# Half of the last FFN's tokens sorted by expert instead of run through all eight experts

## The reference

```python
shared = silu(xf @ shared_w1.T) * (xf @ shared_w2.T) @ shared_w3.T      # hidden 512
scores = sigmoid(xf @ router_w.T)                                       # 8 experts
_, top_idx = top_k(scores + expert_bias, 2)
mask = one_hot(top_idx, 8).sum(axis=-2)
gates = scores * mask
h1, h2 = split(einsum('td,ehd->teh', xf, w12), 2)                       # hidden 128 per expert
h = silu(h1) * h2 * gates[:, :, None]
routed = einsum('teh,edh->td', h, w3)
x = x + 0.5 * (shared + routed)
```

## Time and profile before

| | us |
|---|---|
| median of three runs | 722.5 |
| the profiled execution, device time | 724.5 |
| its span, first to last instruction | 722.5 |
| first FFN, first half (0 to 124 us) | TensorE busy 111.4 of 124.0 |
| mamba, sections 1 to 6 (482.6 to 587.5) | TensorE busy 104.4 of 104.9 |
| mamba, last section (587.5 to 604.6) | TensorE busy 14.7 of 17.1 |
| last FFN, start (604.6 to 616.2) | TensorE busy 10.7 of 11.6 |
| last FFN, units (616.2 to 718.0) | TensorE busy 101.5 of 101.8 |

### The profile page before, as it was taken

One profiled execution on the slowest core, in us unless ns is written; L12 is line 12 of the kernel. 1 busy time (PEld: TensorE's weight loads), 2 busy tenths in 40 slices (PEclk: granted clock), 3 DMA queues, 4 the chain that ended last, 5 costly groups with the idle time before them and its releaser, 6 DMA issues. The chain is left out here.

```text
span 722.5 us, 12386 instructions
## 1 busy us (share of the span) xinstructions
PE 677.4 (94%) x4100; PEld 506.3 (70%) x4100; DVE 569.2 (79%) x1308; ACT 419.3 (58%) x757; POOL 324.5 (45%) x404
## 2 busy tenths in 40 slices
PE   7899998797899999999999878999999998999997
PEld 5667774643457777777778676777777775777785
DVE  5789978989978888988989855666766676879774
ACT  4557686885245555556656647555565555455553
POOL 2568884101227766465658461220413200555463
PEclk9999999999999999999999989999999999999999
DMA  6625430000013232222213100000000000323131
GB/s 168 200 89 187 137 110 1 0 1 0 1 52 125 70 108 90 88 59 81 96 59 90 29 1 1 2 2 2 1 2 0 0 1 2 117 74 118 56 122 44
DMA packets 34329, 43.16 MB, mean 60 GB/s; under 512 B 5216, under 2 KB 17504, under 8 KB 34272
## 3 DMA queue, kind: packets, MB, share of 16 engines
q1 hardware_dynamic: 34272, 42.46, 19.1%
HBM read 41.13 MB, written 1.31 MB: 59 GB/s over the span
## 5 line engine op out<-in xcount | busy, mean ns | idle before, releaser
L697 POOL TENSOR_TENSOR p_prod<-p_p,p_gate_row 128x512 f32<-128x512 f32 x128 | 203.5, 1602 | 108.7 <-DVE p_p L504 62.4
L384 ACT ACTIVATE p_sil<-p_ps_a 128x512 f32<-128x512 f32 x176 | 105.3, 598 | 131.1 <-PE p_ps_a L100 126.8
L509 DVE TENSOR_TENSOR p_hlo<-p_prod,p_hhi 128x512 fp32r<-128x512 f32 x176 | 149.6, 851 | 0.3 <-ACT p_hhi L393 0.2
L504 DVE TENSOR_TENSOR p_p<-p_sil,p_ps_b 128x512 f32<-128x512 f32 x128 | 87.1, 681 | 54.3 <-ACT p_sil L384 37.3
L393 ACT CAST p_hhi<-p_prod 128x512 fp32r<-128x512 f32 x176 | 108.1, 615 | 24.9 <-POOL p_prod L697 24.9
L98 PE MATMUL p_ps_a<-xt_hi,w_uphi 128*128 128x512 f32 x176 | 74.2, 422 | 0.0
L98 PE MATMUL p_ps_acc<-p_hhi,w_downhi 128*128 128x512 f32 x176 | 71.1, 404 | 1.2 <-DVE p_hlo L509 1.0
L98 PE MATMUL p_ps_b<-xt_hi,w_uphi 128*128 128x512 f32 x176 | 71.2, 404 | 0.1
L100 PE MATMUL p_ps_a<-xt_hi,w_uplo 128*128 128x512 f32 x176 | 70.1, 398 | 0.0
L99 PE MATMUL p_ps_a<-xt_lo,w_uphi 128*128 128x512 f32 x176 | 70.1, 398 | 0.0
L100 PE MATMUL p_ps_b<-xt_hi,w_uplo 128*128 128x512 f32 x176 | 69.8, 396 | 0.0
(11 more groups left out here) (355 smaller groups left out, 1432.1 us busy)
## 6 DMA issues: line engine op xcount, KB each, us to landing
p_gate_row<-gate_rows SPq DMA_DIRECT2D x128, 256.0 KB, 3.3
w_rawbuf<-in_L_ffn_fc_w_dram SPq DMA_DIRECT2D x3, 512.0 KB, 7.0
w_rawbuf<-in_L_ffn_w_dram SPq DMA_DIRECT2D x3, 512.0 KB, 6.5
out_dram<-x SPq DMA_DIRECT2D x4, 256.0 KB, 3.5
w_rawbuf<-in_L_ffn_shared_w_dram SPq DMA_DIRECT2D x3, 256.0 KB, 5.8
x<-in_L_attn_x_dram SPq DMA_DIRECT2D x2, 256.0 KB, 3.9
x<-in_L_attn_x_dram SPq DMA_DIRECT2D x1, 512.0 KB, 9.2
mb_xraw<-in_L_attn_W_B_dram SPq DMA_DIRECT2D x1, 512.0 KB, 5.0
```

The costliest lines, as they stand in the source:

```text
L384: nc.scalar.activation(sil[:, u % 2], ps_a[:, u % 2], ACT.Silu).then_inc(c["sil"].sem, 1)
L504: nc.vector.tensor_tensor(dst, sil[:, u % 2], ps_b[:, u % 2], ALU.mult).then_inc(c["p1"].sem, 1)
L509: nc.vector.tensor_tensor(hlo[:, u % R], prod[:, u % R], hhi[:, u % R].bitcast(F32), ALU.subtract).then_inc(c["hlo"].sem, 1)
L697: G.tensor_tensor(prod[:, u % R], p1[:, u % 2], gate_row[:, e % ROWS], ALU.mult).then_inc(c["prod"].sem, 1)
```

## The change

The last FFN has a function of its own, `sparse_stream`. Blocks 2 and 3 are computed as before, by 12 units each. Of blocks 0 and 1 (tiles 0 to 7) only the four shared units are computed so. Their experts are done on sorted rows: each of the 1024 tokens is written twice to DRAM, once for each chosen expert, into a list in which each expert's rows begin at a multiple of 128. The list has 23 tiles (`SLOT_TILES = HALF * 2 + EXPERTS - 1`, always all of them computed), in six groups of up to four tiles. Each tile is read back, turned, multiplied by its own expert's weights (whose place in SBUF TensorE has in a register), and written to a second DRAM list, from which each token's two results are gathered and added to x with their gates.

Parts:

1. In mamba, in the two sections that turn blocks 0 and 1: the router's logits on TensorE (12 matmuls), tanh, `choose` on VectorE. In the last section: ranks on TensorE (9 small matmuls), places on VectorE, and at its end GpSimd scatters tiles 0 to 3 (8 indirect DMAs). The norm of block 2 is there too. The loop is written out, its VectorE, ScalarE, GpSimd and TensorE instructions otherwise in the old order.
2. In the first FFN: a blank for the sorted list, 1.5 MB of zeros, is written to DRAM in SyncE's queue.
3. In the last FFN: eight shared units (g = 0 to 7, `CUT` = 8), during which GpSimd scatters tiles 4 to 7 and TensorE loads 23 registers from SBUF; the six sorted groups; then blocks 2 and 3 (g = 8 to 31). `LEAD` is 4 as before; the ring of hidden tiles is 4. In block 2 the experts' gate products alternate between GpSimd and VectorE; the gathers of the results are on GpSimd between its products. The results are added in block 3.

```diff
+    def scatter(self, j):
+        for k in range(2):
+            self.nc.gpsimd.indirect_dma_start(self.rows_dram[:, :], bass.IndirectOffsetOnAxis(ap=self.place[:, k, j:j + 1], axis=0),
+                                              self.xn[:, j], None).then_inc(self.c["z_scat"].sem, 16)
 # mamba, TensorE, step q == 1 of a section
                         if head is not None:
-                            pe.wait_ge(c["xlo"].sem, c["xlo"].at(head + 1))
+                            sort.logits(pe, head, xt, router, ps_y)
+                            outputs(h, m, 0)
+                            pe.wait_ge(c["gth"].sem, c["gth"].at(head + 1))
+                        if not more:
+                            outputs(h, m, 0)
+                            pe.wait_ge(c["z_slot"].sem, c["z_slot"].at(1))
                         tail.to_tokens(pe, m - 1, ps_y)
 # mamba, VectorE
+                    if q == 3 and head is not None:
+                        sort.choose(dve, head)
+                    if q == 0 and not more:
+                        sort.places(dve, ps_y)
+                        sort.owners(dve)
 # mamba, GpSimd, after its last section
+            pool.wait_ge(c["z_place"].sem, c["z_place"].at(1))
+            pool.wait_ge(c["z_blank"].sem, c["z_blank"].at(16))
+            for j in range(SCATTERED):
+                sort.scatter(j)
 # first FFN, SyncE
         def load_rest(sp):
+            sp.dma_start(rows_dram.rearrange("(t p) c -> p t c", p=P), kept["xraw"][:, 0:1].broadcast_to(
+                [P, SLOT_TILES, P])).then_inc(counts["z_blank"].sem, 16)
             w1_set.load(sp, slice(4, None))
             rw_set.load(sp, slice(0, None))
 # last FFN, TensorE
+            def z_up(s):
...
+                for t in range(sizes(s)):
+                    some = bass.ds(owner[s * BT + t] * 2 + S * 2 * P, 2 * P)
+                    last = three_pass_turned(pe, raised(s)[:, t].rearrange("p a c -> p (a c)"),
+                                             [q[s % 2][:, bass.ts(t, P)] for q in (z_xhi, z_xlo)], [q[:, some] for q in up_flat])
...
+            for g in range(CUT):
+                step(g)                     # g == 2: turn_gates(2); g == 7: z_turn_x(0); after each down: z_owners(g)
+            z_turn_x(1)
+            for s in range(GROUPS):
+                z_up(s)
+                if s:
+                    z_turn_h(s - 1)
+                if s >= 2:
+                    z_down(s - 2)
+                if s + 2 < GROUPS:
+                    z_turn_x(s + 2)
+            step(CUT)
+            z_turn_h(GROUPS - 1)
+            z_down(GROUPS - 2)
+            step(CUT + 1)
+            z_down(GROUPS - 1)
+            for g in range(CUT + 2, UNITS):
+                step(g)
 # last FFN, VectorE: the product of p1 waits for the gate product two experts back
+                    dst = p1[:, g % 2]
+                    after(dve, c["prod"], at_expert(g) - 1)
 # last FFN, GpSimd
+            for j in range(SCATTERED, HALF - 1):
+                sort.scatter(j)
+            scale(3)
+            sort.scatter(HALF - 1)
+            weights(2)
+            weights(3)
+            for h in range(2):
+                kept = c[f"z_kept{h}"]
+                pool.wait_ge(kept.sem, kept.at(16 * (GROUPS // 2)))
+            gathered = 0
+            for g in range(FIRST[2] + S, FIRST[2] + U, 2):
+                while gathered < 3 + (g - FIRST[2] - S) // 2:
+                    sort.gather(gathered, z_back)
+                    gathered += 1
+                weigh(g)
 # last FFN, SyncE: rows(2), wait for the scatters, loads and stores of the groups, rows(3), the four stores of x
```

More of the change, by code:

```diff
@@ L100, in three_pass, with three_pass_turned @@
     return pe.matmul(out, weights[1], moving[0], start=False, stop=stop)
+def three_pass_turned(pe, out, tokens, weights):
+    pe.matmul(out, tokens[0], weights[0], start=True, stop=False)
+    pe.matmul(out, tokens[0], weights[1], start=False, stop=False)
+    return pe.matmul(out, tokens[1], weights[0], start=False, stop=True)
 class FfnKind:
@@ L1613 @@
 SPENT = (RWKV_SEMS + [None] * len(MAMBA_SEMS))[:len(MAMBA_SEMS)]
+SPARSE_SPENT = [n for n in MAMBA_SEMS if n not in ("m_yc", "m_sel", "m_yo", "m_yb", "m_yt", "m_yT", "m_yh", "m_yl", "m_ow", "m_out")]
 class MambaHead:
@@ L1785, in add_out, with mamba_phase @@
         self.nc.vector.tensor_tensor(xb, bank[:, 2:4], xb, ALU.add).then_inc(c["m_out"].sem, 1)
-def mamba_phase(nc, counts, spare, sb, ps, x, xt, consts, w, keep, spent, norm, head, tail):
+def mamba_phase(nc, counts, spare, sb, ps, x, xt, consts, w, keep, spent, norm, head, tail, sort, router):
     c = counts
@@ L1939, in turn_head @@
                 for j in range(BT):
-                    last = pe.transpose(bank[:, j], norm["xn"][:, j], ident[:])
+                    last = pe.transpose(bank[:, j], xraw[:, b * BT + j], ident[:])
                 last.then_inc(c["xt"].sem, 1)
@@ L1951, in section @@
                         if head is not None:
-                            pe.wait_ge(c["xlo"].sem, c["xlo"].at(head + 1))
+                            sort.logits(pe, head, xt, router, ps_y)
[4 more added lines that the diff above has]
+                            pe.wait_ge(c["z_slot"].sem, c["z_slot"].at(1))
                         tail.to_tokens(pe, m - 1, ps_y)
-                    if q:
+                    if q > 1 or q and head is None and more:
                         outputs(h, m, q - 1)
-                    elif not first:
+                    elif not q and not first:
                         outputs(1 - h, m - 1, GROUPS - 1)
@@ L2033, in _ @@
             section(0, 2, group=3)
-            with pe.Fori(0, 2) as i:
+            for i in range(2):
                 section(1, i * 2 + 3)
@@ L2083, in section @@
                         bend(m - 1)
+                        if head is not None:
+                            sort.bend(act, head, ps_y)
                     if q == 3 and not first and more:
@@ L2136, in _ @@
             section(0, 2, group=3)
-            with act.Fori(0, 2) as i:
+            for i in range(2):
                 section(1, i * 2 + 3)
@@ L2216, in normal_head @@
                 for j in range(BT):
-                    last = V.scalar_tensor_tensor(out=norm["xn"][:, j], in0=x[:, b * BT + j], scalar=norm["moments"][:, j, 0:1],
+                    last = V.scalar_tensor_tensor(out=xraw[:, b * BT + j], in0=x[:, b * BT + j], scalar=norm["moments"][:, j, 0:1],
                                                   in1=norm["rstd"][:, j:j + 1].broadcast_to([P, P]), op0=ALU.subtract,
@@ L2297, in _ @@
             section(0, 2, group=3)
-            with dve.Fori(0, 2) as i:
+            for i in range(2):
                 section(1, i * 2 + 3, measured=i)
                 section(0, i * 2 + 4, head=i)
-            section(1, BATCH - 1, more=False)
+            section(1, BATCH - 1, more=False, measured=2)
             silu(BATCH - 1)
@@ L2373, in _ @@
             section(0, 2)
+            sort.prepare(pool)
             pool.wait_ge(c["m_grid"].sem, c["m_grid"].at(10))
-            with pool.Fori(0, 2) as i:
+            for i in range(2):
                 section(1, i * 2 + 3, measured=i)
                 section(0, i * 2 + 4)
-            section(1, BATCH - 1, more=False)
+            section(1, BATCH - 1, more=False, measured=2)
+            pool.wait_ge(c["z_place"].sem, c["z_place"].at(1))
+            pool.wait_ge(c["z_blank"].sem, c["z_blank"].at(16))
+            for j in range(SCATTERED):
+                sort.scatter(j)
         @block.sync
@@ L2544, in program @@
             if stage == "mamba":
-                tail = mamba_stage(head)
-            if stage[:3] == "ffn" and (k == 0 or STAGES[k - 1][:3] != "ffn"):
+                tail, sort = mamba_stage(head)
+            if k + 1 == len(STAGES):
+                sparse_stream(nc, f"p{k}", counts, scoped, ps, x, xt, consts, ffn_kind(stage), gate_dram, norm, sort, tail, out_dram,
+                              flat, kept["zs"], kept["xraw"])
+            elif stage[:3] == "ffn" and (k == 0 or STAGES[k - 1][:3] != "ffn"):
                 stages = [stage]
```

673 lines of the change are left out of this document (669 added, 4 removed).

## The result

| | us |
|---|---|
| before, median of 4 runs beside it | 721.88 (721.24 to 723.5) |
| after, median of 4 runs | 740.77 (739.43 to 741.76) |
| ratio, 95% interval | 1.0257 (1.0231 to 1.0283) |
| the profiled execution of after, its span | 741.76, 740.0 |
| its mean TensorE clock (before) | 0.972 (0.987) |

The kernel is slower by 2.6%, some 19 us; 735.2 us with 718 to 747 was forecast. The two profiled spans differ by 17.5 us: the last FFN's first matmul starts 6.2 us later (610.78, before 604.6), and from there to the end it takes 129.2 us where it took 117.9, 11.3 more.

What follows compares the result with a forecast made beforehand. TensorE was taken to bound the last FFN and mamba, except mamba's last section, paced by a ring of VectorE, ScalarE and TensorE. Costs of 28.7 against 16.0 gave +12.7 us, so 735.2 us, range 718 to 747.

Steps and rivals of the forecast that it cites:

- A: Last FFN, blocks 0 and 1: TensorE loses expert units and router, gains 23 sorted tiles; -16.0 us, the whole gain.
- B: Mamba: logits, waits in their sections, the last section's VectorE work and block 2's norm cost 7.9 us.
- Scatters: Mamba's end: GpSimd's 8 scatters at 1.04 us each, 8.3 us, fit in 10.9; at 1.63 they outlast it by 2.1.
- C: First FFN: block 2's gates wait behind the blank in SyncE's queue, making TensorE late by 4.6 us.
- D: Last FFN: TensorE's 23 register loads from SBUF, at 0.14 us each, cost 3 us (bounds 0 and 9.2).
- The rival that priced each load as a stall: Last FFN: each register load stalls TensorE by the longest gap, 9.2 us instead of 3.0; about 741 us, chance 0.14.
- E: Last FFN, step 2: TensorE waits for block 2's gates, weighted by GpSimd; 2.0 us (bounds 0 and 4).
- F: Last FFN, sorted groups: wait to turn group 1 (1.5 us) plus register arithmetic (1.0); 2.5 us in all.
- G: Last FFN, entry to block 2: TensorE waits for GpSimd's product behind stored results, six gathers; 7.3 us (4.1 to 10.9).
- H: Last FFN: a TensorE stand of 7 us costs one more stretch at half clock; 1.4 us (bounds 0 and 3).
- the faster case: GpSimd's indirect DMAs cost 0.5 us; E and most of H go, G falls to 4.1; about 718 us, chance 0.16.
- the dear one: Indirect DMAs at 1.63 us each: 2.1 at mamba's end, 1.2 in E, 3.6 in G; about 742 us, chance 0.12.

Runs made afterwards that it cites:

- e8: Changed kernel with block 2's products on VectorE, its gates turned later, mamba's statistics moved, additions placed where GpSimd has no product, and smaller moves: 718.85 us, ratio 0.9942.
- e10: Changed kernel with the three small instructions of the tiles' owners done three times over in mamba's last section: 746.22 us.
- e7: Changed kernel with block 2's statistics and the tiles' owners one step later in mamba's last section: 742.44 us.
- e6: Changed kernel with a second blank of the same size behind the first in SyncE's queue of the first FFN: 747.04 us.
- e1: Changed kernel without VectorE's 16 additions of gathered results in block 3: 734.56 us.
- e2: Changed kernel with the same 16 additions, one in each of 16 steps instead of two in each of 8: 736.57 us.
- e9: Kernel of e8 with the first two sorted groups' rows read before block 2's gate rows, and register loads spread over other steps: 718.36 us.
- e5: Changed kernel without TensorE's 23 register loads, each sorted tile taking a fixed expert's weights: 742.05 us.
- e3: Changed kernel with all gate products of block 2 on VectorE and GpSimd's 16 gathers issued together: 733.13 us.
- e4: Changed kernel with block 2's gates transposed one step later in the last FFN: 738.01 us.

## Why the prediction was right, and where it was wrong

The direction, mamba's part, the stand at block 2 and its cause were right. The forecast was 5.6 us short (4.6 against the profiled execution), and that it was no more is luck: its terms were 14.2 us too low in four places and 9.4 too high in four others. The rivals' 741 and 742 lie nearer to the measured 740.8, and neither of their mechanisms is there. By its own terms:

- **A, -16.0.** Right as far as it can be read: the small matmuls start 0.12 and 0.11 us apart (648.72, 648.84), the groups' tiles and their transposes cost what they were priced, and units in the full stretches are 2.10 apart. Without the stalls the gain is there: e8's last FFN is 11.9 us shorter than before, with holes of 0.83, 1.33 and 0.80 us left in it, and a clock of 0.91 from 637 to 657 (1.8); less the 1.4 of the old half clock at the start, which is gone, that makes some 15.
- **B, 7.9.** The stage ended 6.7 later from its own start (6.2, and mamba began 0.5 earlier). The logits start 0.11 apart. The sections with them grew by 2.2 and 2.1, priced at 1.8 each. The last section grew by 3.3 (19.20 against 15.89), priced at 3.7, and e10 shows that VectorE's work is paid there in full, e7 that moving it by a step saves 0.3. Written out, the loop cost nothing: the section without logits between these two is 0.4 shorter.
- **Scatters.** 0.96 us and 1.26 from start to start: near the 1.04 taken, but the 0.30 us of issue between two was not in the sum. Eight ended at 610.7, with the stage.
- **C, 4.6: failed, 0.7.** The step that failed is "the blank, 1.5 MB at 211 GB/s, adds 7.1 us". 211 GB/s was what the stretch asked for, not what the engines can move: the kernel after moved 338 GB/s from 58 to 60 us. The queue was 4.3 us later, the product 1.75, TensorE 0.7. With a second blank (e6) the cover was used up and TensorE paid 4.2.
- **D, 3.0: failed in size, 0.9 to 1.1.** I spread the cost over 23 loads; it shows once here, twice in e1, e2 and e10 (1.8 together in e1). Three loads take some 1.7 us of the sequencer's time (an estimate: 1.89 less what it needs to issue), four 2.4 at most in e9 (631.70 to 634.08). Most lie beside the 2.1 us of up and down product queued ahead. The rule on `tensor_load` in the Trainium skill ("DMA: Bandwidth & Descriptors", section "Latency and other measured facts"), about 600 ns, agrees with the 0.55 to 0.6 us per load that this makes. The rival that priced each load as a stall, 9.2 in all, is refuted.
- **E, 2.0: 2.7.** Right in cause, and I had no clock loss behind it. Both ends of the wait came sooner than I had counted, TensorE at 15.1 us into the stage (17.6), the weights at 17.8 (20.0), and the two errors cancel.
- **F, 2.5.** The prologue 1.49 as priced; nothing for register arithmetic (e5).
- **G, 7.3: 9.4.** The stored results landed after 2.3 us instead of 3.5; the six gathers took 7.3 instead of 6.2, because of the 0.30 between them; what stands behind the gate product took 1.5 instead of 0.7, since TensorE's next matmul is the first expert's down product and waits for VectorE's gate product and low half (685.55 to 687.09); and TensorE was through its queued work 1.0 sooner, at 677.3 + 0.4. e3 showed the cause: the stand and its clock are gone, 10.0 us.
- **H, 1.4: failed, 5.6.** The old half clock at the start of the stage went (-1.4). Three new ones came: 6.5 us at 0.52 behind the gates (3.1), the nine matmuls behind the stand (1.8), and 728.5 to 735.5 at 0.53 (eleven steps of 0.43 for 0.233, 2.1). I had given the stand one such loss, and a wait of 2 us none. The 3.1 is not firm: in e1, e2 and e10, the same kernel up to there, the half clock behind the gates lasts five matmuls instead of twelve, and yet the second sorted group is turned only 0.0 to 0.4 us sooner (37.0 to 37.3 us into the stage, after 37.4), as the second hole of e5's section comes out.
- **Left out: the additions, 6 to 7.** Seven units at 0.91 more make 6.4. e1 gives 7.9, but with the 2.1 of the last half clock, which stands in H. What is left of the spans' difference for this term is 7.2: -16.0 + 6.7 (B) - 0.5 (mamba's start, C in it) + 0.9 + 2.7 + 1.5 + 9.4 + 5.6 + 7.2 = 17.5. So the sum closes by this term, and some 0.8 of it is shown by no row. Between C's 0.7 and mamba's start lies 1.2 us that no part of the change accounts for; the kernel before had a clock of 0.84 from 130 to 140 us in its profile, the kernel after one of 1.00. The prediction says that results are added in block 3 and never prices them. It counted GpSimd's and VectorE's work as shares of a stage, where both have room; it is the overlap in time that costs, and VectorE then sets the pace of a stage which was TensorE's. Too low were this term (7.2), H (4.2), G (2.1) and E (0.7); too dear were C (5.1, with mamba's start), D (2.1), B (1.2) and F (1.0), which hid most of it.
- **Rivals.** An indirect DMA costs neither 0.5 nor 1.63, so the faster case and the dear one both fall: 718 was not within reach by GpSimd's price alone. Its own terms don't give it either: E and H gone and G at 4.1 leave costs of 22.1 against 16.0, about 729.
- **Signs.** Right were the stand before block 2's experts (9.4 us for 7), mamba's last section (19.2 for 20), the groups (3.6 for 3.5) and a later gate row (69.0 for 72). Wrong was the first: TensorE's time from the last FFN's first matmul to its last was to fall by under 8; it grew by 10.9 (113.8, now 124.7). The prediction's own terms for the last FFN add up to +0.2, so that sign didn't follow from them.

## What to carry to other kernels

Price each new instruction on the engine where it stands and against what runs beside it at that moment: an addition of 0.35 us cost 1.4 beside a GpSimd pass. Put indirect DMAs and waits for DRAM behind, never ahead of, products that TensorE needs soon, and the loads that a sequencer must do where matmuls are queued ahead of it. A wait of 2.7 us on TensorE cost up to twice its length here, as the clock halved behind it, so small waits are worth moving first.

## What the runs showed of the hardware that was not expected

- An addition (VectorE, 128x128, all operands in SBUF) takes 0.34 us alone and 1.37 to 1.39 when issued 0.4 us into a GpSimd product of 1.63; it ends 0.14 us behind the product (e2). It works the other way too: the product takes 1.27 us with VectorE idle (684.28) and 1.63 when issued 0.2 us into VectorE's low half (713.02 and 712.80), which reads two SBUF tiles. So some 0.35 us of most such products (median 1.63, least 1.27, in the kernel before too) looks like a stand as well; no run isolates it. The final addition from PSUM (0.68 us at 710.39, product running) didn't wait. Beside GpSimd's gathers additions ran at full speed.
- An indirect DMA of 128 rows costs GpSimd 0.95 us and 0.30 before the next, scatter or gather alike, and up to 1.4 while VectorE has its gate products (1.39 at 694.28 in e3).
- A wait of 2.7 us and a hole of 0.9 put TensorE to 1.2 GHz, for 6 us in the kernel after, for under 3 in e1 and e2 behind the same wait; a wait of 0.6 and a hole of 1.05 did not (e4). The mean clock also fell to 0.66 over 5 us in mamba in three of the profiles (e3, e7, e8, 575 to 580), where TensorE was busy throughout, and over 5 us of mamba's end in three others (e4 and e5 from 600, e6 from 605); why is open.
- 1.5 MB of plain writes move a shared queue by 4.3 to 4.7 us (e6), above 300 GB/s.
